# A median search with sixteen marks in six rounds instead of eight marks in eight rounds, in a kernel of three gated norms and a column scan

## The chip, the cores and the metric

One Trainium2 chip, of which this kernel uses one core. The metric is the device time of one execution in microseconds (us), taken as the median of three timed runs. The core has five engines that run their own instruction streams and meet only through semaphores: TensorE (PE in the profile, PEld for its weight loads), VectorE (DVE), ScalarE (ACT), GpSimd (POOL) and SyncE (SP), which here issues all DMAs. Data lie in two on-chip memories of 128 partitions: SBUF, and PSUM, into which TensorE writes and which GpSimd doesn't use here.

## The reference

The input `x` has shape 4 x 1024 x 32 x 32 (images, channels, height, width), in float32. Three times over, `x` is group-normalized, and a gate of one number for each image and channel is computed and applied:

```python
xf = x.reshape(b, c, h * w)
u = jnp.stack([mean(xf), max(xf), std(xf, ddof=1)], axis=-1)   # [4, 1024, 3]
med = jnp.median(u.reshape(b, -1), axis=-1)                   # one per image, over 3072 values
u = (u - med) ** 3
z = jnp.einsum('bck,ck->bc', u, cfc_w) / sqrt(1 + BN_EPS) * bn_w + bn_b
return x * sigmoid(z)                                          # and x = x + this, over _gn(x)
```

Then a fourth layer runs 62 dependent steps over the columns, forward and back: each takes the column before it, multiplies its 1024 channels by a 1024 x 1024 matrix, adds a bias, applies a leaky ReLU and adds the column's own input.

## The kernel before, in words

`x` stays in SBUF as `x_sb[128, 8, 32, 128]`: channel within a tile, 8 channel tiles, 32 columns, 4 images x 32 rows. The execution has three stages.

**Loading, to about 48 us of the profile.** SyncE loads `x` in sixteen pieces of about 1 MB. GpSimd first writes its constants (L330 to L397: identity, group masks, and the constants of the median search), then adds pairs of columns (`pair_add`, L400) as the pieces land; TensorE sums them (L585, L597), VectorE takes maxima (L846), ScalarE sums squares (L469). The weight matrix is loaded behind `x`.

**Three gate layers, 48 to 110 us.** Only the statistics, three numbers per image and channel, are worked on. They lie in `unit[128, 4, 3, 8]`. Each layer runs in a chain: `first_norm` or `next_norm` on VectorE makes `unit`; `median(layer)` finds the median of each image; the cube, the weights and the sigmoid make the gate (L1047 to L1055, L517).

**The scan, from 111 us to the end.** Every column step is 48 large matmuls for the two halves (L680, L683, L686), with weights split into a high part `w_hi` and a low part `w_lo`. The split itself is done inside the gate layers: ScalarE copies the high part (`split_high`, L494), GpSimd subtracts it to make the low part in 24 pieces of a third of a tile (`split_low`, L428), eight per layer. TensorE waits for all 24 at L668 before it warms up for the scan.

**How the median is found.** There are 3072 values for each image. They must stand so that a partition can compare many of them with one threshold. So the statistics are first copied into four columns of `x_sb` that aren't needed then (`COPY_COL`, the last four; SyncE loads them again at L307 once the last layer's values are spread), each value repeated once for every mark: VectorE copies the means (L1042), ScalarE the maxima (L507), GpSimd the deviations (L448). TensorE transposes these columns, 128 values at a time, into PSUM (`ps_values`, L630). After that a partition stands for one pair of image and mark, in one of `SHARES` shares of the channels, and along it lie its values, half of them for ScalarE (`ps_halves[0]`) and half for VectorE (`ps_halves[1]`): `EACH` values for each.

A round then goes like this. ScalarE sums the signs of (threshold - value) over its half (L499, with an accumulator read behind it), VectorE counts the values below the threshold in its half (L998, likewise). GpSimd does one `split_low` beside them. TensorE adds the counts over the partitions that belong to each mark with two small matmuls (L641 waits for ScalarE, L643 for VectorE), and then runs four idle matmuls (`keep_warm`, L578). VectorE compares the sums with half the number of values and adds up the moves of the thresholds (L1009); its signal `thr_ready` starts the next count on both engines, and the next `split_low`. With M marks, a round narrows the interval to 1/M. `SEARCH_WIDTH` is 2.0, and after the last round it is 2 / 8^8.

The last round has another end: one matmul group (`ps_last`, L648 to L656) gives the floors of the two middle ranks, VectorE makes them (L1017, L1019), masks the statistics below each floor (L1022, L1024) and takes the nearest value above (L1026); two small matmuls with a reduction between them give the median to all partitions (L660, L1033, L664).

In layers 1 and 2, three small VectorE operations for the next norm are put into the first three rounds, behind the count (L1002, L1004, L1007). In layer 0, GpSimd folds parameters behind its last `split_low` of that layer (`fold_params`, L431: eight small operations), and VectorE waits for them at L1050.

Of the kernel before, what the change touches and what calls it, by code (L numbers as in the profile page):

```python
# [6 lines left out]
def gated_norm_and_column_scan_kernel(nc, x_cols, w_t, gate_params, conv_bias, prelu_slope, out_cols):  # L7
# [17 lines left out]
    N = 4  # L25
# [21 lines left out]


    SEARCH_LO, SEARCH_WIDTH = -149 / 256, 2.0
    MARKS = 8  # L50
    SHARES = P // (N * MARKS)
    ROUNDS = 8
    STEP = [SEARCH_WIDTH / MARKS ** (k + 1) for k in range(ROUNDS)]
    MARKED = N * MARKS
    TERMS = MARKED + 2
# [8 lines left out]
    with ctx:  # L64
# [86 lines left out]
        both_shift = sb("both_shift", [P, N, CT])  # L151

        spreading = ExitStack()
        ps_values = spreading.enter_context(nc.psum_tensor("ps_values", [P, 2 * 512], fp32))
        spreading.close()
        ps_prods = pb("ps_prods", [P, 2 * HALF])
        ps_prod = [ps_prods[:, c * HALF:(c + 1) * HALF] for c in range(2)]
# [2 lines left out]
        ps_below = pb("ps_below", [P, 2 * 512])  # L160
        ps_group = pb("ps_group", [P, 512])
        ps_means = ps_group[:, N * CT:2 * N * CT]
        ps_cells = [ps_group[:, 128 + 64 * r:128 + 64 * r + TERMS] for r in range(2)]
        ps_last = ps_below[:, 512:512 + 2 * N * (MARKS + 1)]
        ps_second = pb("ps_second", [P, 512])
        ps_var = ps_second[:, 0:N * CT]
# [105 lines left out]

        def copies(k):

            pair = x_sb[:, k, COPY_COL:COPY_COL + 2, :].rearrange("p w m -> p (w m)")
            each = unit[:, :, k, :].rearrange("p n c -> p c n").unsqueeze(3).broadcast_to([P, CT, N, MARKS])
            return pair.rearrange("p (c n j) -> p c n j", n=N, j=MARKS), each

        def copied(t):

            return x_sb[:, t // 2, COPY_COL + t % 2, :]

        moves = stage[:, HALF:HALF + ROUNDS * TERMS].rearrange("p (k t) -> p k t", k=ROUNDS)
        moved = cells[:, 0:TERMS]
        last_moved = tall[:, :, :, :].rearrange("p n k c -> p (n k c)")[:, 0:2 * N * (MARKS + 1)]            .rearrange("p (u n j) -> p u n j", u=2, n=N)
        ps_halves = [ps_values[:, r * 512:r * 512 + EACH] for r in range(2)]

        act_signs = stage[:, 0:EACH // 2].bitcast(bf16)

# [39 lines left out]
        def _(pool):  # L329
# [30 lines left out]
                .then_inc(masks_started, 1)  # L360
            pool.wait_ge(masks_started, 7)
            pool.tensor_tensor(places[:, :], places[:, :], eights[:, :], ALU.mult).then_inc(masks_started, 1)
            pool.tensor_tensor(own[:, :], eights[:, 0:2 * N], eights[:, 2 * N:4 * N], ALU.add).then_inc(masks_started, 1)
            pool.tensor_tensor(cells[:, :], ident[:, 0:2 * MARKED], ident[:, 2 * MARKED:4 * MARKED], ALU.add)\
                .then_inc(masks_started, 1)
            started = 10
            for width in (8, 4, 2, 1):
                pool.wait_ge(masks_started, started)
                pool.tensor_tensor(places[:, 0:width], places[:, 0:width], places[:, width:2 * width], ALU.add)\
                    .then_inc(masks_started, 1)  # L370
                started += 1
            pool.tensor_tensor(own[:, 0:N], own[:, 0:N], own[:, N:2 * N], ALU.add).then_inc(masks_started, 1)
            pool.tensor_tensor(cells[:, 0:MARKED], cells[:, 0:MARKED], cells[:, MARKED:2 * MARKED], ALU.add)\
                .then_inc(masks_started, 1)
            for t in (cell_once, cell_twice):
                pool.memset(t[:, MARKED:TERMS], 0.0).then_inc(consts_ready, 1)
            for t in (last_once, last_twice, next_rank):
                pool.memset(t[:, :, :, :], 0.0).then_inc(masks_started, 1)
            pool.memset(last_moves[:, :, :, :], STEP[-1]).then_inc(consts_ready, 1)
            pool.wait_ge(masks_started, started + 5)  # L380
            by_mark = cells[:, 0:MARKED].rearrange("p (n j) -> p n j", n=N)
            for t, weight in ((cell_once, 1.0), (cell_twice, 2.0)):
                pool.tensor_scalar(t[:, 0:MARKED], cells[:, 0:MARKED], weight, 0.0, ALU.mult, ALU.add)\
# [61 lines left out]
            for layer in range(LAYERS):  # L445

                pool.wait_ge(unit_ready, 2 * layer + 2)
                pool.tensor_copy(*copies(2)).then_inc(pool_copied, 1)  # L448
                pool.wait_ge(spread_high, layer + 1)
                split_low()  # L450
                for k in range(1, ROUNDS):
                    pool.wait_ge(thr_ready, layer * (ROUNDS - 1) + k)
                    split_low()
                if layer == 0:
                    fold_params()

# [2 lines left out]
        def _(act):  # L459
# [35 lines left out]

            def count_signs(layer, k):

                with nc.allow_low_precision(reason="whole numbers up to 384 are exact in float16"):
                    act.activation(act_signs, ps_halves[0], ACT.Sign, bias=moves[:, k, MARKED:MARKED + 1], scale=-1.0,  # L499
                                   accum_out=balance[:, k:k + 1]).then_inc(act_counted, 1)  # L500

# [72 lines left out]
        def _(pe):  # L574
# [28 lines left out]
            for layer in range(LAYERS + 1):  # L603
# [16 lines left out]
                if layer > 0:  # L620
                    keep_warm(6, ps_warm)
                keep_warm(8, ps_warm)
                for t in range(2 * NSTAT):
                    if t == 0:
                        pe.wait_ge(dve_copied, layer + 1)
                    elif t == 2:
                        pe.wait_ge(act_copied, layer + 1)
                    elif t == 4:
                        pe.wait_ge(pool_copied, layer + 1)
                    last = pe.transpose(ps_halves[t // NSTAT][:, t % NSTAT * P:(t % NSTAT + 1) * P], copied(t), ident[:, :])  # L630
                    if t == NSTAT - 1:
                        last.then_inc(spread_low, 1)
                last.then_inc(spread_high, 1)

# [161 lines left out]
        def _(dve):  # L796
# [192 lines left out]
            def median(layer):  # L989

                values = unit[:, :, :, :].rearrange("p n k c -> p n (k c)")

                dve.wait_ge(spread_high, layer + 1)
                for k in range(ROUNDS):
                    if k > 0:
                        dve.wait_ge(thr_ready, layer * (ROUNDS - 1) + k)
                    with nc.allow_low_precision(reason="whole numbers up to 384 are exact in float16"):
                        dve.tensor_scalar(below_flags[:, :], ps_halves[1], moves[:, k, MARKED:MARKED + 1], 0.0,  # L998
                                          ALU.is_lt, ALU.add, accum_out=below[:, k:k + 1]).then_inc(dve_counted, 1)
                    if k < ROUNDS - 1:  # L1000
                        if layer > 0 and k == 0:
                            dve.tensor_tensor(t1[:, 0, :, :], cent[:, 1, :, :], cent[:, 1, :, :], ALU.mult)  # L1002
                        if layer > 0 and k == 1:
                            dve.scalar_tensor_tensor(t2[:, 0, :, :], cent[:, 3, :, :], (PIX - 1.0) / PIX,  # L1004
                                                     cent[:, 3, :, :], ALU.mult, ALU.mult)
                        if layer > 0 and k == 2:
                            dve.tensor_tensor(cent[:, 0, :, :], t1[:, 0, :, :], t2[:, 0, :, :], ALU.add)  # L1007
                        dve.wait_ge(cells_counted, layer * (ROUNDS - 1) + k + 1)
                        dve.scalar_tensor_tensor(moved, ps_cells[k % 2], COUNT_LIMIT, moves[:, k, :],  # L1009
                                                 ALU.is_le, ALU.mult,  # L1010
                                                 accum_out=moves[:, k + 1, MARKED:MARKED + 1]).then_inc(thr_ready, 1)

                dve.wait_ge(lows_given, layer + 1)
                link(dve.tensor_scalar(last_moves[:, :, :, MARKS], ps_lows.unsqueeze(1).broadcast_to([P, 2, N]),
                                       -STEP[-1], None, ALU.add))
                dve.wait_ge(floors_ready, layer + 1)
                link(dve.scalar_tensor_tensor(last_moved, ps_last.rearrange("p (u n j) -> p u n j", u=2, n=N),  # L1017
                                              COUNT_LIMIT, last_moves[:, :, :, :], ALU.is_le, ALU.mult))
                link(dve.tensor_reduce(floors[:, :, :], last_moved, AX.X, ALU.add))  # L1019

                each = values.unsqueeze(1).broadcast_to([P, 2, N, VALUES])
                link(dve.tensor_tensor(spread[:, :, :, :], each,  # L1022
                                       floors[:, :, :].unsqueeze(3).broadcast_to([P, 2, N, VALUES]), ALU.is_lt))
                link(dve.scalar_tensor_tensor(spread[:, :, :, :], spread[:, :, :, :], -BIG, each,  # L1024
                                              ALU.mult, ALU.subtract))
                dve.tensor_reduce(tops[:, :].rearrange("p (u n) -> p u n", u=2),  # L1026
                                  spread[:, :, :, :], AX.X, ALU.max)\
                    .then_inc(tops_ready, 1)
                dve.wait_ge(params_loaded, 48)
                dve.tensor_copy(cube[:, :, NSTAT, :],  # L1030
                                params[:, layer, NSTAT + 1, :].unsqueeze(1).broadcast_to([P, N, CT]))
                dve.wait_ge(tops_turned, layer + 1)
                dve.tensor_reduce(middle[:, :], ps_mid[0:2 * N, 0:P], AX.X, ALU.max).then_inc(median_ready, 1)  # L1033
                dve.wait_ge(median_spread, layer + 1)
# [199 lines left out]
```

## Time and profile before

| | us |
|---|---|
| median of 3 runs (lowest, highest) | 865.32 (865.29, 865.5) |
| the profiled execution, its own time | 865.18 |
| its span, first to last instruction | 863.5 |
| TensorE busy in the span | 840.1 (97%) |
| VectorE busy | 659.0 (76%) |
| ScalarE busy | 412.7 (48%) |
| GpSimd busy | 67.4 (8%), all of it before 102 us |

The granted TensorE clock is 1.000 of full over the span. The scan is TensorE's: busy tenths of 9 in every slice from about 110 us. Between 48 and 110 us the large matmuls don't run yet, and what TensorE is busy with there is mostly `keep_warm`: 173 matmuls of L578, 42.8 us. A timeline row has the start, the duration, the engine, the line, the operation, output <- input, and in brackets the idle time of the engine before it and what ended it. Durations of neighbours on one engine overlap, since an instruction is still finishing when the next one starts; the distance of two starts is what counts.

### The profile page before, as it was taken

Reading aid. Unit: us, or ns where it says so; the run is one execution under the profiler, and the core shown is the slowest. Engines: PE = TensorE matmul, PEld = TensorE weight load, DVE = VectorE, ACT = ScalarE, POOL = GpSimd, SP = SyncE. Lnnn points to the kernel's source line nnn. Section 1 sums busy time; section 2 is a strip of 40 time slices with the busy share of each in tenths; the row PEclk is TensorE's granted clock in tenths of the full one; section 3 lists DMA queues with packets and bytes.
Section 4 is the critical chain, followed back from the end, with each engine's and each line's share of the span. In section 5 each row is a group of like instructions: output and inputs, shape, how many; then the busy total and the mean of one; then the engine's idle time right before and its main releaser. Section 6 shows DMA issues by size and latency. Waiting matters only on the chain.

```text
span 863.5 us, 13836 instructions
## 1 busy us (share of the span) xinstructions
PE 840.1 (97%) x4078; PEld 664.7 (77%) x4078; DVE 659.0 (76%) x1446; ACT 412.7 (48%) x1375; POOL 67.4 (8%) x106
## 2 busy tenths in 40 slices
PE   7788999999999999999999999999999999999998
PEld 7743478888888888888888888888888888888886
DVE  6977787767667676676766787788877888778887
ACT  6964325444454445444454444544445444454444
POOL 8963300000000000000000000000000000000000
PEclk9999999999999999999999999999999999999999
DMA  9940200000000000000000023331333223332233
GB/s 376 418 184 1 97 26 1 0 0 0 0 0 0 0 0 0 0 0 0 0 0 0 15 83 97 97 93 59 92 97 97 87 60 96 97 97 77 68 97 98
DMA packets 70654, 56.34 MB, mean 65 GB/s; under 512 B 1904, under 2 KB 66416, under 8 KB 68720
## 3 DMA queue, kind: packets, MB, share of 16 engines
q1 hardware_dynamic: 70640, 56.17, 19.5%
q8 instruction: 7, 0.11, 0.1%
q14 instruction: 7, 0.06, 0.0%
HBM read 39.39 MB, written 16.78 MB: 65 GB/s over the span
## 4 chain that ended last, share of the span: by engine, by line
PE 89%; POOL 4%; DVE 4%; ACT 2%; issue 1%; POOLq 0%; DVEq 0%
PE ps_prods L680 27%; PE ps_prods L683 27%; PE ps_prods L686 27%; PE ps_turns L702 6%; POOL pairs L400 3%; ACT stage L499 1%; PE ps_below L578 1%; DVE cells L1009 1%; PE ps_below L597 0%; DVE below_flags L998 0%; PE ps_group L641 0%; PE ps_values L630 0%; POOL stage L393 0%; POOL stage L396 0%; PE ps_second L660 0%
## 5 line engine op out<-in xcount | busy, mean ns | idle before, releaser
L680 PE MATMUL ps_prods<-w_hi,s_hi 128*128 128x512 f32 (+1 forms) x1000 | 404.4, 404 | 0.6 <-DVE s_hi L1154 0.6
L683 PE MATMUL ps_prods<-w_lo,s_hi 128*128 128x512 f32 (+1 forms) x1000 | 403.0, 403 | 0.0
L686 PE MATMUL ps_prods<-w_hi,s_lo 128*128 128x512 f32 (+1 forms) x1000 | 392.8, 393 | 0.0
L526 ACT ACTIVATE act_buf<-ps_prods 128x256 f32<-128x256 f32 x247 | 81.5, 382 | 354.4 <-PE ps_prods L686 354.4
L1102 DVE SCALAR_TENSOR_TENSOR x_sb<-act_buf,x_sb 128x256 f32 (+1 forms) x247 | 105.1, 426 | 153.6 <-ACT act_buf L533 143.8
L680 PEld LDWEIGHTS ps_prods<-w_hi,s_hi 128*128 128x128 f32 x1000 | 188.4, 188 | 40.0 <-DVE s_lo L1160 1.3
L686 PEld LDWEIGHTS ps_prods<-w_hi,s_lo 128*128 128x128 f32 x1000 | 188.9, 189 | 38.2
L683 PEld LDWEIGHTS ps_prods<-w_lo,s_hi 128*128 128x128 f32 x1000 | 189.2, 189 | 32.4
L533 ACT ACTIVATE act_buf<-ps_turns,bias 128x128 f32<-128x128 f32 x494 | 156.6, 377 | 51.5 <-PE ps_turns L702 51.5
L539 ACT ACTIVATE ps_below<-ps_turns,neg_bias 128x128 f32<-128x128 f32 x494 | 152.2, 362 | 0.0
L1109 DVE SCALAR_TENSOR_TENSOR x_sb<-ps_below,neg_slope,x_sb 128x256 f32 (+1 forms) x247 | 118.9, 481 | 5.3
L1077 DVE TENSOR_TENSOR s_lo<-x_sb,s_hi 128x256 fp32r<-128x256 f32 x244 | 103.8, 426 | 8.4
L702 PEld LDWEIGHTS ps_turns<-ident,act_buf 128*128 128x128 f32 x494 | 69.0, 140 | 33.1
L702 PE MATMUL ps_turns<-ident,act_buf 128*128 128x128 f32 x494 | 93.9, 272 | 0.0
L1071 DVE TENSOR_SCALAR s_hi<-x_sb 128x256 fp32r (+1 forms) x244 | 70.8, 290 | 4.2
L578 PE MATMUL ps_below<-ones_bf 128*128 128x512 bf16 x173 | 42.8, 379 | 0.0
L1142 DVE TENSOR_TENSOR x_sb<-x_sb,stage 128x1024 f32 (+1 forms) x31 | 38.0, 1225 | 3.2
L1135 DVE TENSOR_TENSOR stage<-stage,a_shift 128x1024 f32<-128x1024 f32 x31 | 38.0, 1225 | 1.1
L1065 DVE TENSOR_TENSOR x_sb<-x_sb,g_shift 128x1024 f32 (+1 forms) x31 | 38.0, 1225 | 1.1
L1062 DVE TENSOR_TENSOR x_sb<-x_sb,g_scale 128x1024 f32 (+1 forms) x31 | 37.8, 1219 | 0.0
L1132 DVE TENSOR_TENSOR stage<-stage,a_scale 128x1024 f32<-128x1024 f32 x31 | 37.8, 1218 | 0.0
L846 DVE TENSOR_REDUCE half_max<-x_sb 128x4 f32<-128x2048 f32 (+1 forms) x16 | 35.4, 2214 | 0.0
(186 smaller groups left out, 342.1 us busy)
## 6 DMA issues: line engine op xcount, KB each, us to landing
stage<-x_cols SPq DMA_DIRECT2D x31, 512.0 KB, 4.1
out_cols<-x_sb SPq DMA_DIRECT2D x31, 512.0 KB, 4.8
x_sb<-x_cols SPq DMA_DIRECT2D x15, 1024.0 KB, 18.6
w_raw<-w_t SPq DMA_DIRECT2D x8, 512.0 KB, 19.4
x_sb<-x_cols SPq DMA_DIRECT2D x1, 2048.0 KB, 8.2
x_sb<-x_cols SPq DMA_DIRECT2D x2, 512.0 KB, 27.1
out_cols<-x_sb SPq DMA_DIRECT2D x4, 128.0 KB, 2.1
params<-gates SPq DMA_DIRECT2D x1, 60.0 KB, 14.3
```

Of the source, the lines that this page charges most:

```text
L526: act.activation(act_buf[:, half], ps_prod[c if bank is None else bank][:, half], ACT.Copy) .then_inc(raw_copied, 1)
L533: last = act.activation(act_buf[:, (2 * r + j) * P:(2 * r + j + 1) * P], ps_turn[r][:, j * P:(j + 1) * P], ACT.Identity, bias=bias[:, ct:c ...
L539: last = act.activation(ps_below[:, r * 512 + j * P:r * 512 + (j + 1) * P], ps_turn[r][:, j * P:(j + 1) * P], ACT.Relu, bias=neg_bias[:, c ...
L578: pe.matmul(bank[:, :], ones_bf[:, :], ones_bf[:, :].unsqueeze(1).broadcast_to([P, 4, P]), start=True, stop=True)
L680: pe.matmul(out, s_hi[:, k, :], w_hi[:, k, w_cols], start=(k == 0), stop=False)
L683: pe.matmul(out, s_hi[:, k, :], w_lo[:, k, w_cols], start=False, stop=False)
L686: return pe.matmul(out, s_lo[:, k, :], w_hi[:, k, w_cols], start=False, stop=(k == CT - 1))
L702: last = pe.transpose(ps_turn[r][:, j * P:(j + 1) * P], act_buf[:, q * P:(q + 1) * P], ident[:, :])
L1071: dve.tensor_scalar(s_hi[:, ct0:ct0 + 2, :], pair, 1.0, None, ALU.mult)\
L1077: dve.tensor_tensor(s_lo[:, ct0:ct0 + 2, :], pair, s_hi[:, ct0:ct0 + 2, :].bitcast(fp32), ALU.subtract).then_inc(state_ready, 1)
L1102: dve.scalar_tensor_tensor(col, y, 0.0, col, ALU.max, ALU.add).then_inc(above_added, 1)
L1109: dve.scalar_tensor_tensor(col, below, neg_slope[:, 0:1], col, ALU.mult, ALU.add)\
```

## The change

`MARKS` goes from 8 to 16, `ROUNDS` from 8 to 6. The final interval is the same, 2 / 16^6 = 2 / 8^8. Everything sized by them follows:

- `SHARES` goes from 4 to 2, `EACH` from 384 to 768, `TERMS` from 34 to 66, `STEP` has six entries.
- The copies are 128 x 512 for each statistic instead of 128 x 256, over all four columns of `COPY_COL`, and there are twelve transposes in each layer instead of six; `ps_values` takes four PSUM banks of 512 instead of two, ScalarE's half starting at 0 and VectorE's at 1024. `spread_low` is signalled behind the sixth transpose, `spread_high` behind the twelfth.
- `ps_last`, `last_moves`, `last_once` and the like are 136 wide instead of 72. `last_moved` moves from `tall` to `spread`.
- GpSimd's constants: `places` is added up in three steps instead of four, `own` and `cells` lose their second addition, and there are ten instructions for `moves` (L393, L396) instead of fourteen.
- GpSimd's eight pieces of `w_lo` per layer stay eight. Six of them are still started by the rounds; the other two follow directly behind the sixth, in a new loop, in layer 0 ahead of `fold_params`.

```diff
-    MARKS = 8
+    MARKS = 16
-    ROUNDS = 8
+    ROUNDS = 6
...
-        ps_values = spreading.enter_context(nc.psum_tensor("ps_values", [P, 2 * 512], fp32))
+        ps_values = spreading.enter_context(nc.psum_tensor("ps_values", [P, 4 * 512], fp32))
...
-        ps_cells = [ps_group[:, 128 + 64 * r:128 + 64 * r + TERMS] for r in range(2)]
+        ps_cells = [ps_group[:, 128 + 128 * r:128 + 128 * r + TERMS] for r in range(2)]
...
-            pair = x_sb[:, k, COPY_COL:COPY_COL + 2, :].rearrange("p w m -> p (w m)")
+            pair = x_sb[:, k, COPY_COL:COLS, :].rearrange("p w m -> p (w m)")
...
-            return x_sb[:, t // 2, COPY_COL + t % 2, :]
+            return x_sb[:, t // 4, COPY_COL + t % 4, :]
...
-        ps_halves = [ps_values[:, r * 512:r * 512 + EACH] for r in range(2)]
+        ps_halves = [ps_values[:, r * 1024:r * 1024 + EACH] for r in range(2)]
...
-            pool.tensor_tensor(own[:, :], eights[:, 0:2 * N], eights[:, 2 * N:4 * N], ALU.add).then_inc(masks_started, 1)
-            pool.tensor_tensor(cells[:, :], ident[:, 0:2 * MARKED], ident[:, 2 * MARKED:4 * MARKED], ALU.add)\
+            pool.tensor_tensor(own[:, 0:N], eights[:, 0:N], eights[:, N:2 * N], ALU.add).then_inc(masks_started, 1)
+            pool.tensor_tensor(cells[:, 0:MARKED], ident[:, 0:MARKED], ident[:, MARKED:2 * MARKED], ALU.add)\
...
-            for width in (8, 4, 2, 1):
+            for width in (4, 2, 1):
...
                 for k in range(1, ROUNDS):
                     pool.wait_ge(thr_ready, layer * (ROUNDS - 1) + k)
                     split_low()
+                for _ in range(W_THIRDS // LAYERS - ROUNDS):
+                    split_low()
                 if layer == 0:
                     fold_params()
...
-                for t in range(2 * NSTAT):
+                half = EACH // P
+                for t in range(2 * half):
                     if t == 0:
                         pe.wait_ge(dve_copied, layer + 1)
-                    elif t == 2:
+                    elif t == 4:
                         pe.wait_ge(act_copied, layer + 1)
-                    elif t == 4:
+                    elif t == 8:
                         pe.wait_ge(pool_copied, layer + 1)
-                    last = pe.transpose(ps_halves[t // NSTAT][:, t % NSTAT * P:(t % NSTAT + 1) * P], copied(t), ident[:, :])
-                    if t == NSTAT - 1:
+                    last = pe.transpose(ps_halves[t // half][:, t % half * P:(t % half + 1) * P], copied(t), ident[:, :])
+                    if t == half - 1:
                         last.then_inc(spread_low, 1)
                 last.then_inc(spread_high, 1)
```

## Rows read from the trace of the kernel before

**Rows 1.** The page, its chain that ended last: shares of the span by engine.
```profile
PE 89%; POOL 4%; DVE 4%; ACT 2%; issue 1%; POOLq 0%; DVEq 0%
```

**Rows 2.** Timeline, one round of layer 2: start us, duration us, engine, line, operation.
```profile
99.31 0.20 DVE L1009 SCALAR_TENSOR_TENSOR cells<-ps_group,stage 128x34 f32<-128x34 f32 x1 [0.35 <-PE ps_group L643]
...
99.55 0.58 ACT L499 ACTIVATE stage<-ps_values,stage 128x384 bf16<-128x384 f32 x1 [0.54 <-DVE cells L1009]
99.55 0.62 DVE L998 TENSOR_SCALAR_CACHE_REDUCE below_flags<-ps_values,stage 128x384 uint8<-128x384 f32 x1
...
100.03 0.20 ACT L499 ACTIVATION_READ_ACCUMULATOR stage<-ps_values,stage 128x1 f16 x1
100.09 0.09 DVE L998 DVE_READ_ACCUMULATOR below_flags<-ps_values,stage 128x1 f16 x1
...
100.53 0.19 DVE L1009 SCALAR_TENSOR_TENSOR cells<-ps_group,stage 128x34 f32<-128x34 f32 x1 [0.35 <-PE ps_group L643]
```

**Rows 3.** Timeline, the start of the search in layer 1.
```profile
71.79 0.29 DVE L1042 COPY x_sb<-unit 128x256 f32<-128x256 f32 x1
...
71.94 0.40 POOL L448 COPY x_sb<-unit 128x256 f32<-128x256 f32 x1 [6.70 <-DVE unit L838]
...
72.16 0.84 PE L630 MATMUL ps_values<-ident,x_sb 128*128 128x128 f32 x6
...
73.13 0.62 DVE L998 TENSOR_SCALAR_CACHE_REDUCE below_flags<-ps_values,stage 128x384 uint8<-128x384 f32 x1 [0.76 <-PE ps_values L630]
...
73.67 0.09 DVE L998 DVE_READ_ACCUMULATOR below_flags<-ps_values,stage 128x1 f16 x1
...
74.05 0.20 DVE L1009 SCALAR_TENSOR_TENSOR cells<-ps_group,stage 128x34 f32<-128x34 f32 x1
```

**Rows 4.** Groups by line and shape: busy us, mean ns of one.
```profile
L1030 DVE COPY cube<-params 128x32 f32<-128x32 f32 x3 | 0.6, 186 | 0.0
...
L1042 DVE COPY x_sb<-unit 128x256 f32<-128x256 f32 x3 | 0.9, 287 | 0.0
...
L1077 DVE TENSOR_TENSOR s_lo<-x_sb,s_hi 128x256 fp32r<-128x256 f32 x244 | 103.8, 426 | 8.4
...
L1135 DVE TENSOR_TENSOR stage<-stage,a_shift 128x1024 f32<-128x1024 f32 x31 | 38.0, 1225 | 1.1
...
L930 DVE TENSOR_TENSOR grow<-gate,rstd 128x32 f32<-128x32 f32 x3 | 0.6, 192 | 0.9 <-ACT gate L517 0.9
...
L469 ACT ACTIVATE ps_prods<-x_sb,mean_div 128x1024 f32<-128x1024 f32 x16 | 17.6, 1098 | 0.0
```

**Rows 5.** Timeline, the end of the search in layer 2.
```profile
100.81 0.91 POOL L428 TENSOR_TENSOR w_lo<-w_raw,w_hi 128x342 fp32r<-128x342 f32 x1 [0.30 <-DVE cells L1009]
...
101.84 0.23 DVE L1017 SCALAR_TENSOR_TENSOR tall<-ps_below,last_moves 128x72 f32<-128x72 f32 x1 [0.36 <-PE ps_below L656]
102.11 0.23 DVE L1019 TENSOR_REDUCE floors<-tall 128x8 f32<-128x72 f32 x1
102.37 0.36 DVE L1022 TENSOR_TENSOR spread<-unit,floors 128x192 f32<-128x192 f32 x1
```

**Rows 6.** Timeline, GpSimd and VectorE side by side, in layer 0 and layer 2.
```profile
64.03 0.38 POOL L437 TENSOR_SCALAR neg_bias<-bias 128x8 f32<-128x8 f32 x1
...
93.50 0.91 POOL L428 TENSOR_TENSOR w_lo<-w_raw,w_hi 128x342 fp32r<-128x342 f32 x1 [0.33 <-DVE cells L1009]
...
94.00 0.46 DVE L1004 SCALAR_TENSOR_TENSOR t<-cent 128x32 f32<-128x32 f32 x1
```

**Rows 7.** Timeline of GpSimd alone, the loading stage.
```profile
9.46 0.22 POOL L393 TENSOR_SCALAR stage<-own 128x32 f32<-128x32 f32 x1
...
10.02 0.22 POOL L393 TENSOR_SCALAR stage<-own 128x32 f32<-128x32 f32 x1
...
26.77 19.77 POOL L400 TENSOR_TENSOR pairs<-x_sb 128x1024 f32<-128x1024 f32 x9 [1.19 <-DMA x_sb<-x_cols]
```

**Rows 8.** Busy time in one stretch: PE, PEld, DVE, ACT, POOL, then granted clock, DMA share, GB/s.
```profile
23.40:29.30 5.90, 4.10 (x33) 3.75 (x33) 5.90 (x5) 4.56 (x9) 4.58 (x3) 1.00 1.01 417
```

More of the change, by code:

```diff
@@ L279, in copied @@
         def copied(t):
[L281 removed]
+            return x_sb[:, t // 4, COPY_COL + t % 4, :]
         moves = stage[:, HALF:HALF + ROUNDS * TERMS].rearrange("p (k t) -> p k t", k=ROUNDS)
         moved = cells[:, 0:TERMS]
[L285 to L286 removed]
+        last_moved = spread[:, :, :, :].rearrange("p u n v -> p (u n v)")[:, 0:2 * N * (MARKS + 1)]\
+            .rearrange("p (u n j) -> p u n j", u=2, n=N)
+        ps_halves = [ps_values[:, r * 1024:r * 1024 + EACH] for r in range(2)]
         act_signs = stage[:, 0:EACH // 2].bitcast(bf16)
@@ L371, in _ @@
                 started += 1
-            pool.tensor_tensor(own[:, 0:N], own[:, 0:N], own[:, N:2 * N], ALU.add).then_inc(masks_started, 1)
-            pool.tensor_tensor(cells[:, 0:MARKED], cells[:, 0:MARKED], cells[:, MARKED:2 * MARKED], ALU.add)\
-                .then_inc(masks_started, 1)
             for t in (cell_once, cell_twice):
@@ L379, in _ @@
             pool.memset(last_moves[:, :, :, :], STEP[-1]).then_inc(consts_ready, 1)
-            pool.wait_ge(masks_started, started + 5)
+            pool.wait_ge(masks_started, started + 3)
             by_mark = cells[:, 0:MARKED].rearrange("p (n j) -> p n j", n=N)
@@ L496, in count_signs @@
             def count_signs(layer, k):
-                with nc.allow_low_precision(reason="whole numbers up to 384 are exact in float16"):
+                with nc.allow_low_precision(reason="whole numbers up to 768 are exact in float16"):
                     act.activation(act_signs, ps_halves[0], ACT.Sign, bias=moves[:, k, MARKED:MARKED + 1], scale=-1.0,
@@ L996, in median @@
                         dve.wait_ge(thr_ready, layer * (ROUNDS - 1) + k)
-                    with nc.allow_low_precision(reason="whole numbers up to 384 are exact in float16"):
+                    with nc.allow_low_precision(reason="whole numbers up to 768 are exact in float16"):
                         dve.tensor_scalar(below_flags[:, :], ps_halves[1], moves[:, k, MARKED:MARKED + 1], 0.0,
```

## The prediction

> **What bounds the kernel now.** I read the chain that ended last first: TensorE has 89% of it, and GpSimd, VectorE and ScalarE share the rest [rows 1]. The 89% is the scan, which the change doesn't touch: what matters is when it starts. I therefore went to the timeline of the gate layers. There the work is a chain across engines, none of them full, and each step starts when the one before it ends. In a round [rows 2] the reader is to see both counts start at 99.55, ScalarE's done at 100.23 (100.03 + 0.20) and VectorE's at 100.18; the sums come back to L1009 at 100.53, and the next count starts 0.24 us after L1009 (99.31 to 99.55). A round is 1.22 us (99.31 to 100.53), of which the count is 0.68. Everything that lengthens this chain moves the end of the kernel one to one, since TensorE waits for the gate before it can start the scan. So the change is judged by the length of three searches.
>
> Times below go by the profiled execution, 865.18 us (span 863.5); the median of the runs is 865.32, 0.14 above it.
>
> **The counts.** Each count reads 768 values instead of 384. What does a value more cost? On VectorE, 1024 against 256 elements take 1225 against 426 ns [rows 4]: 1.04 ns each, so +0.40 us. The count's own row gives the upper bound, 0.62 us over 384, 1.6 ns each, +0.62 us [rows 2]; the lower bound is the rate of the copies, 0.45 ns (186 ns for 32, 287 ns for 256 elements, [rows 4]), +0.17 us. I take 1.04, because the count reads PSUM and its 0.54 us to the accumulator read is hardly to be had at the copy's rate. On ScalarE, a sum over 1024 elements takes 1098 ns [rows 4], the count over 384 580 ns [rows 2]: 0.81 ns each, I take +0.32 us (upper bound 1.5 ns from the count's row alone, +0.58).
>
> VectorE then ends its count 0.63 + 0.40 = 1.03 us after the start, ScalarE 0.68 + 0.32 = 1.00. They are near level, and VectorE becomes the later one. From the end of VectorE's count to L1009, where it is the last, takes 0.29 us (73.76 to 74.05, [rows 3]). The matmuls are 66 columns instead of 34, for which I add 0.01, and L1009 has 32 elements more, 0.03. A round becomes 1.03 + 0.29 + 0.01 + 0.24 + 0.03 = 1.60 us.
>
> **One layer, step by step.**
> - Copy (L1042): 256 elements more at 0.45 to 0.53 ns, +0.13 us [rows 4]; it stands before the first transpose. ScalarE's and GpSimd's copies grow too, but are wanted only at the fifth and ninth transpose. GpSimd's lasts 0.40 us now and ends at 72.34 [rows 3]; even doubled it ends at 72.74, while the ninth transpose starts about 0.13 + 8 x 0.11 us after 72.16, at 73.2. Cost nothing; uncovered it would be 0.4 at most.
> - Transposes: six take 0.84 us with 0.27 for the last alone, a distance of 0.11 us [rows 3]. Six more: +0.68. VectorE waits for the last one, as it does now at 73.13.
> - First count, to the first L1009: +0.40 + 0.01 = +0.41.
> - Six distances from L1009 to L1009 at 1.22 go (7.31 in all), four at 1.60 come (6.40): -0.91.
> - Last count: from the last L1009 to L1017. Now 1.31 us (100.53 to 101.84, [rows 2, 5]). ScalarE's end moves by 0.32 and VectorE's end by 0.40 from a start 0.05 earlier, so +0.35; 0.03 for L1009; the matmuls with 136 columns are within this rounding: +0.38.
> - L1017 and L1019 have 64 elements more each, 0.067 us each: +0.13.
>
> Sum: 0.13 + 0.68 + 0.41 - 0.91 + 0.38 + 0.13 = +0.82 us for a layer, +2.5 for three. Two rounds are saved, 2.4 us, but six counts cost 0.32 to 0.40 more each, and the wider copy and transposes 0.8. This is the main term.
>
> **GpSimd's two late pieces.** The change leaves the eight pieces of `w_lo` and starts three of them at the last `thr_ready`. The last count starts at 100.77 (L1009 at 100.53 [rows 2] plus 0.24). Now the last piece starts 0.04 us after it and is over at 101.72, before L1017 [rows 5]. Three at 0.91 end at 0.04 + 2.73 = 2.77 us after the count's start. VectorE reaches L1022 after 1.60 us now (102.37 - 100.77), with the terms above after 1.60 + 0.35 + 0.13 = 2.08 us: in the middle of the third piece. What happens when a VectorE instruction meets one of these, [rows 6] show: L1004, a 32-element instruction whose like takes 192 ns alone [rows 4], takes 0.46 us, and ends at 94.46, 0.05 after the GpSimd piece at 94.41. I found six such meetings (L1002, L1004, L1007 and the L838 that writes `rstd`, in layers 1 and 2, the first three with `w_lo`), and all end 0.04 to 0.05 us behind GpSimd. The counts run beside the pieces undisturbed: L998 has 0.62 us with a piece beside it from its start [rows 2]. So L1022 waits. It ends at 2.77 + 0.05 + 0.17 (160 elements more than the 32 of those rows) = 2.99 us instead of 2.08 + 0.36 = 2.44: +0.55. GpSimd's pieces may overlap by some 0.04 each in their records, which would make it 0.47; I take +0.5 for each layer, +1.5. At the least it costs nothing (rival below). At the most the third piece itself starts late behind L1017 and pushes the rest by another 0.3, +0.8 for each layer.
>
> The Trainium skill (SBUF — State Buffer, "Who interferes with whom") states that a VectorE instruction with two SBUF inputs contends with a GpSimd instruction that reads SBUF, and that the later one is blocked for the whole instruction, while reductions and instructions with one SBUF input are left alone. By that, L1017 (one input from PSUM) and L1019 (a reduction) pass and L1022 is the one that waits; the six meetings agree, since all have two SBUF inputs. If L1017 waited as well, the end of the third piece would still set L1022, and the sum would stay.
>
> In layer 0 `fold_params` now comes behind the third piece, eight small instructions. L1022 and L1024 run there, and one waits for the other: L437, 8 elements, took 0.38 us beside L1022 [rows 6]. I add 0.15 us once. The fold ends some 2 us behind the third piece, near 4.9 us after the last count's start; L1052, which needs it, comes at about 5.4 us, so it is just covered; uncovered it would be up to 0.5 once.
>
> **The constants.** GpSimd saves four `moves` instructions, 0.56 us for a pair (9.46 to 10.02, [rows 7]), and three small additions, 1.7 us, less some 0.5 for wider ones. It reaches its first `pair_add` about 1 us sooner, and the chain that ended last runs through it. But at 26.77 GpSimd had sat idle for 1.19 us until a piece of `x` landed [rows 7], and it can't start that piece before it has landed: that swallows the gain. I take 0, bounds 0 and -1.0.
>
> **Other covers.** `w_lo` is complete at about 104.7 + 0.8 us in layer 2, and TensorE asks for it behind the last gate, at 107.5 now: covered. The reload of four columns of `x` starts later with the last transpose and has 8.2 us to land; it is wanted after 111. Cost nothing.
>
> **Sum.** 865.18 + 2.5 + 1.5 + 0.15 = 869.3 in the profiled execution; the median of the runs stands 0.14 above it, so **869.4 us**, 0.47% slower.
>
> **The rivals.**
> - B, no lock: the pieces never meet L1022, because they overlap more or the counts are longer. Then the searches cost 2.5 us alone: 867.7. For it: three meetings with `w_lo` are few, all with small instructions. Against: all agree, and the times overlap by 0.7 us.
> - C, rounds with a fixed price (the other side): if a count of 768 cost no more than one of 384, two saved rounds would come through. For it: of 0.62 us some is start-up. A layer would be 0.13 + 0.68 + 0.01 - 2.44 (two rounds) + 0.16 (the wider L1009 and matmuls), and the end at L1022 still hangs on the third piece, 2.99 us against 1.96 now, +1.03: -0.43, so 865.18 - 1.3 + 0.15 = 864.0; without the lock 861.5. It decides below +0.09 us for a count with the lock and +0.2 without; the rates of both engines [rows 2, 4] say 0.3 to 0.4.
> - D, the clock falls: a longer round leaves TensorE about 0.5 us idle behind its four warm-up matmuls, where it was 0.1. If the granted clock fell to 1.2 GHz in the searches, twelve transposes would cost 1.3 us more and the small matmuls 0.2: +1.5 a layer, 871 in one layer to 874 in all. Against: in the loading stage TensorE was busy 4.10 of 5.90 us, and the granted clock was 1.00 [rows 8]; the new round has about 1.2 of 1.6.
> - E, the constants' gain comes through: 868.3. Against it stands the idle time on the DMA.
>
> **How the numbers follow.** My forecast 0.62, B 0.18, E 0.08, D 0.08, C 0.04. What can be told from no change is 0.2%, 1.7 us to either side of 865.32. B, D and E lie above it. Slower 0.92, within 0.2% 0.05 (half of C and counts cheaper than I think), faster 0.03. The range reaches down past B and leaves out C, up to the lock's upper bound and a clock that falls in one layer: 867.3 to 870.9.
>
> **What would show it.** In the profile after: L998 at about 1.02 us and L499 at 0.90; L1009 to L1009 at 1.60; twelve transposes in 1.5 us; from L1042 to L1017 0.7 us more than the 10.87 of now (71.79 to 82.66); L1022 longer than 0.8 us, ending 0.2 behind a GpSimd piece; the clock at 1.00. L998 below 0.8 us would make the forecast wrong on the side of C, L1022 at 0.36 us on that of B.

## The result, and the profile after

The changed kernel takes 870.91 us (median of four executions, 869.52 to 871.78), the kernel before 865.31: a ratio of 1.0062, 95% interval 1.0048 to 1.0075. (The ratios here are estimated from all the executions, so they can differ a little from the quotient of two medians, which is 1.0065 here.) It is slower by 5.6 us. The profiled execution is the fastest of the four, 869.52 us with a span of 867.8, 4.34 us above the one of before. Its granted clock was 1.000; the other three had 0.996, 0.994 and 0.996 over their span. So there are two things to explain: 4.3 us in the profile, and 1.4 more in the median.

To read the first, one stretch is taken out of each trace: from VectorE's first copy of statistics in layer 0 (L1042 before, L1043 after) to its first instruction of the scan (L1150 before, L1151 after). It holds the three searches and nothing of the loading or the scan. Before, it is 57.47 us (52.67 to 110.14); after, 61.24 us (52.64 to 113.88). That is 3.77 us. The load ended at the same moment, and the rest, 0.6 us, lies in the scan, where nothing was changed. The two ends of the stretch, in the timeline of the kernel before:

```profile
52.67 0.28 DVE L1042 COPY x_sb<-unit 128x256 f32<-128x256 f32 x1
...
110.14 0.29 DVE L1150 TENSOR_TENSOR stage<-x_sb,g_scale 128x128 f32<-128x128 f32 x1
```

and in that of the changed kernel:

```profile
52.64 0.42 DVE L1043 COPY x_sb<-unit 128x512 f32<-128x512 f32 x1
...
113.88 0.29 DVE L1151 TENSOR_TENSOR stage<-x_sb,g_scale 128x128 f32<-128x128 f32 x1
```

One round of layer 2, in the timeline of the changed kernel, to be laid beside [rows 2]:

```profile
98.50 0.23 DVE L1010 SCALAR_TENSOR_TENSOR cells<-ps_group,stage 128x66 f32<-128x66 f32 x1 [0.20 <-PE ps_group L644]
...
98.77 0.90 ACT L499 ACTIVATE stage<-ps_values,stage 128x768 bf16<-128x768 f32 x1 [0.60 <-DVE cells L1010]
98.78 1.02 DVE L999 TENSOR_SCALAR_CACHE_REDUCE below_flags<-ps_values,stage 128x768 uint8<-128x768 f32 x1
...
99.57 0.20 ACT L499 ACTIVATION_READ_ACCUMULATOR stage<-ps_values,stage 128x1 f16 x1
99.72 0.09 DVE L999 DVE_READ_ACCUMULATOR below_flags<-ps_values,stage 128x1 f16 x1
...
100.10 0.23 DVE L1010 SCALAR_TENSOR_TENSOR cells<-ps_group,stage 128x66 f32<-128x66 f32 x1 [0.20 <-PE ps_group L644]
```

From L1010 to L1010 it is 1.60 us (98.50 to 100.10), and VectorE (99.81) is now later than ScalarE (99.77). The 384 values more cost VectorE 0.40 us and ScalarE 0.32.

The start of the search in layer 1, against [rows 3]:

```profile
73.01 0.42 DVE L1043 COPY x_sb<-unit 128x512 f32<-128x512 f32 x1
...
73.16 0.74 POOL L446 COPY x_sb<-unit 128x512 f32<-128x512 f32 x1 [6.07 <-DVE unit L839]
...
73.49 1.53 PE L631 MATMUL ps_values<-ident,x_sb 128*128 128x128 f32 x12
...
75.14 1.02 DVE L999 TENSOR_SCALAR_CACHE_REDUCE below_flags<-ps_values,stage 128x768 uint8<-128x768 f32 x1 [1.19 <-PE ps_values L631]
```

The twelve transposes take 1.53 us instead of 0.84, and VectorE sits idle for 1.19 us in front of its count instead of 0.76. GpSimd's copy is done at 73.90 and delays nothing.

The end of the search in layer 1, against [rows 5]:

```profile
83.17 2.64 POOL L426 TENSOR_TENSOR w_lo<-w_raw,w_hi 128x341 fp32r<-128x341 f32 x3 [0.68 <-DVE cells L1010]
...
84.57 0.30 DVE L1018 SCALAR_TENSOR_TENSOR spread<-ps_below,last_moves 128x136 f32<-128x136 f32 x1 [0.34 <-PE ps_below L657]
84.91 0.29 DVE L1020 TENSOR_REDUCE floors<-spread 128x8 f32<-128x136 f32 x1
85.23 0.78 DVE L1023 TENSOR_TENSOR spread<-unit,floors 128x192 f32<-128x192 f32 x1
...
86.85 0.39 PE L661 MATMUL ps_second<-ident,tops 128*8 128x128 f32 x2 [0.88 <-DVE tops L1027]
```

GpSimd's three pieces end at 85.81. L1023 has the same 192 elements as L1022 before, at 0.36 us; here it takes 0.78 and ends at 86.01, 0.20 behind GpSimd. L1018 and L1020 passed through the same pieces and show only their 64 elements more.

The loading stage: GpSimd's first additions start 0.9 us sooner, at 10.71, and it is stopped by DMAs again at 24.30, where before it was stopped at 26.77 [rows 7].

```profile
10.71 12.31 POOL L398 TENSOR_TENSOR pairs<-x_sb 128x1024 f32<-128x1024 f32 x5 [0.32 <-DMA x_sb<-x_cols]
24.30 22.22 POOL L398 TENSOR_TENSOR pairs<-x_sb 128x1024 f32<-128x1024 f32 x10 [1.28 <-DMA x_sb<-x_cols]
```

### The profile page after: what moved, and what is told of

Its sections match the earlier page's. It is cut to its first block, busy times and chain, and to the rows that moved or that the text cites. A ratio compares the mean times of both kernels' runs of the same rounds, so it can differ in the third digit from the quotient of the medians.

```text
span 867.8 us, 13745 instructions
## 1 busy us (share of the span) xinstructions
PE 837.1 (96%) x4060; PEld 664.2 (77%) x4060; DVE 662.8 (76%) x1422; ACT 416.0 (48%) x1363; POOL 67.4 (8%) x99
## 4 chain that ended last, share of the span: by engine, by line
PE 89%; DVE 3%; POOL 3%; ACT 2%; DMA 1%; issue 1%; SPq 0%; POOLq 0%; DVEq 0%
PE ps_prods L681 27%; PE ps_prods L687 27%; PE ps_prods L684 27%; PE ps_turns L703 6%; POOL pairs L398 3%; ACT stage L499 2%; DMA x_sb<-x_cols 1%; PE ps_below L578 1%; PE ps_values L631 1%; PE ps_below L597 0%; DVE cells L1010 0%; DVE below_flags L999 0%; PE ps_group L642 0%; DVE spread L1023 0%; SPq L299 0%
## 5 line engine op out<-in xcount | busy, mean ns | idle before, releaser
L578 PE MATMUL ps_below<-ones_bf 128*128 128x512 bf16 x149 | 36.8, 379 | 0.0
```

The source lines that it names most:

```text
L578: pe.matmul(bank[:, :], ones_bf[:, :], ones_bf[:, :].unsqueeze(1).broadcast_to([P, 4, P]), start=True, stop=True)
```

## The experiments

Chips differ here: the median of the kernel before is 864.9 or 865.0 us on two of them and 866.1 to 866.4 on a third, mostly at a granted clock of 0.999 or 1.000. So each time is given with the kernel before on the same chip (866.06 and 866.39 are two sets on the third). The stretch is the one defined above, in the profiled execution.

| kernel | median us | before, same chip | ratio (95%) | stretch us | executions with a clock under 0.999 |
|---|---|---|---|---|---|
| changed, again | 870.02 | 866.06 | 1.0047 (1.0034 to 1.0061) | 61.25 | 3 of 5 |
| five idle matmuls | 869.55 | 866.06 | 1.0039 (1.0025 to 1.0052) | 61.24 | 1 of 5 |
| piece moved ahead | 868.75 | 866.06 | 1.0036 (1.0023 to 1.0050) | 60.82 | 5 of 5 |
| both | 867.44 | 864.93 | 1.0029 (1.0017 to 1.0040) | 59.98 | 1 of 7 |
| half the counts | 863.66 | 864.93 | 0.9985 (0.9976 to 0.9994) | 56.12 | 1 of 10 |
| and six transposes | 861.56 | 864.93 | 0.9960 (0.9945 to 0.9976) | 54.15 | 0 of 4 |
| before, pieces late | 867.43 | 864.93 | 1.0027 (1.0017 to 1.0037) | 59.90 | 0 of 8 |
| before, two idle matmuls | 869.01 | 866.06 | 1.0034 (1.0022 to 1.0046) | 59.91 | 6 of 6 |
| three idle matmuls | 869.60 | 866.39 | 1.0043 (1.0030 to 1.0056) | 62.97 | 2 of 6 |
| two in the last round | 868.87 | 864.97 | 1.0045 (1.0031 to 1.0059) | 61.27 | 2 of 5 |
| all three mendings | 867.33 | 864.97 | 1.0028 (1.0017 to 1.0038) | 59.94 | 0 of 8 |

**Half the counts.** Both engines read 384 of the 768 values; the other half of the values is left out of all comparisons.

```diff
-act.activation(act_signs, ps_halves[0], ACT.Sign, ...
+act.activation(act_signs[:, 0:EACH // 2], ps_halves[0][:, 0:EACH // 2], ACT.Sign, ...
-dve.tensor_scalar(below_flags[:, :], ps_halves[1], ...
+dve.tensor_scalar(below_flags[:, 0:EACH // 2], ps_halves[1][:, 0:EACH // 2], ...
```

> The changed kernel with both counts over the first 384 of their 768 values; the other half of the values is left out of every comparison, so the medians are wrong. All else (twelve transposes, 512-wide copies, 66 and 136 columns, pieces) stays. Theory 1: a round falls from 1.60 to 1.27 us (four of them), the first count by 0.40, and the last count gives nothing, since L1023 hangs on the third GpSimd piece: 1.7 us for each layer, 5.2 in all, 864.4. Theory 1 without the hold-up at the end: 2.07 a layer, 863.3. Rival C (a count costs the same whatever its length): 869.5.

The stretch is 5.12 us shorter than in the changed kernel, where 5.2 was expected with the hold-up at the end and 6.2 without. The timeline of layer 0 shows both sides: a round is 1.27 us (56.94 to 58.21), and L1023 takes 1.10 us. It arrives sooner and waits longer for the same GpSimd piece. (The row of POOL shows the last two of the three pieces, since this view starts at 62.)

```profile
56.94 0.23 DVE L1010 SCALAR_TENSOR_TENSOR cells<-ps_group,stage 128x66 f32<-128x66 f32 x1 [0.37 <-PE ps_group L644]
...
58.21 0.23 DVE L1010 SCALAR_TENSOR_TENSOR cells<-ps_group,stage 128x66 f32<-128x66 f32 x1 [0.37 <-PE ps_group L644]
...
61.93 1.78 POOL L426 TENSOR_TENSOR w_lo<-w_raw,w_hi 128x341 fp32r<-128x341 f32 x2
...
62.82 1.10 DVE L1023 TENSOR_TENSOR spread<-unit,floors 128x192 f32<-128x192 f32 x1
```

**And six transposes.** The same, and of each half only the three transposes that are still read.

```diff
+if t % half >= half // 2:
+    continue
 last = pe.transpose(...)
-if t == half - 1:
+if t == half // 2 - 1:
     last.then_inc(spread_low, 1)
```

> As the kernel with half the counts, and only the six transposes whose values are still read (the copies stay 512 wide; half the values are left out of every comparison). Theory 1: 6 x 0.11 = 0.68 us less for each layer, 2.0 us under the kernel with half the counts, 862.3. Rival (transposes hide beside other work): no difference between the two.

1.97 us less in the stretch, 2.10 in the medians. The transposes lie bare on the chain, at 0.11 us each.

**Piece moved ahead.** The test of GpSimd's part in the changed kernel.

```diff
 pool.tensor_copy(*copies(2)).then_inc(pool_copied, 1)
+split_low()
 pool.wait_ge(spread_high, layer + 1)
 split_low()
...
-for _ in range(W_THIRDS // LAYERS - ROUNDS):
+for _ in range(W_THIRDS // LAYERS - ROUNDS - 1):
```

> The changed kernel with one of GpSimd's two late pieces started behind its copy, ahead of the wait for the transposes. Two pieces are left at the last round; they end 1.8 us after the last count's start, 0.3 before VectorE asks for L1023. Theory 1 with the lock: L1023 at 0.36 us instead of 0.78, 0.42 to 0.46 us less in each layer, 868.2 at clock 1.000. Rival (the pieces have no part in it, the time is all in the wider steps): 869.5 as before. Theory 2b (clock falls through the idle TensorE at the end of the search, which shrinks from 0.9 to 0.45 us) expects the spread over executions to go; 2a expects it to stay.

L1024 (the L1023 of the changed kernel) is back at 0.36 us in all layers:

```profile
L1024 DVE TENSOR_TENSOR spread<-unit,floors 128x192 f32<-128x192 f32 x3 | 1.1, 359 | 0.1
```

The stretch fell by 0.43 us only, though, since in this profiled execution the clock fell in layer 1 (its rows stand under three idle matmuls, below). With the clock held (the run "both", below) it is 59.98, 1.26 under the changed kernel: 0.42 for each layer. The clock fell in all five executions, so the shorter idle time at the end of the search (theory 2b) did not keep it up.

**Before, pieces late.** The same thing put into the kernel before.

```diff
 pool.wait_ge(thr_ready, layer * (ROUNDS - 1) + k)
-split_low()
+if k not in (5, 6):
+    split_low()
+for _ in range(2):        # behind the loop over k
+    split_low()
```

> The kernel before the change, with the GpSimd pieces of rounds 5 and 6 put behind the one of the last round, so that three run in a row there, as in the changed kernel; nothing else is altered. Theory 1 with the lock: the third piece ends 2.68 us after the last count's start, and L1022 ends 0.21 behind it at 2.89 instead of 1.96: 0.93 us for each layer, 2.8 in all, some 0.15 more in layer 0, 868.2 at clock 1.000. Rival (no lock): 865.3. Theory 2b expects here a granted clock below 1.000 in some executions, since TensorE idles about 1.3 us at the end of each search.

+2.43 us in the stretch, +2.50 in the medians: 0.81 for each layer where I expected 0.93. The rows of layer 0 show why it is a little less. GpSimd began 0.15 us later than usual; L1025 (the old L1022) got in as the second piece ended, the third piece had to wait for it, and it was the next instruction, L1027, that then waited for the third piece:

```profile
62.93 2.76 POOL L428 TENSOR_TENSOR w_lo<-w_raw,w_hi 128x342 fp32r<-128x342 f32 x3 [2.90 <-DVE cells L1012]
...
64.34 0.58 DVE L1025 TENSOR_TENSOR spread<-unit,floors 128x192 f32<-128x192 f32 x1
64.96 0.94 DVE L1027 SCALAR_TENSOR_TENSOR spread<-spread,unit 128x192 f32<-128x192 f32 x1
```

Theory 2b alone is out: TensorE idled for 1.13 us at the end of the search here, and the clock was 0.999 or 1.000 in all eight executions. So an idle end of the search does not bring the clock down by itself, with rounds of 1.22 us.

**The changed kernel once more, and the clock.**

> The changed kernel once more, unaltered. Theory 1 (the sum: counts, transposes, copies and a VectorE instruction held up by GpSimd's late pieces give a fixed +4.3 us) expects 869.5 in every execution whose granted clock is 1.000. Theory 2 (the clock falls in some executions, because TensorE now idles about 0.5 us in each round and 0.9 us at the end of a search) expects single executions at 870.5 to 872 with a mean clock of 0.993 to 0.997, and others at 869.5 with 1.000. If all five are within 0.3 us of each other, theory 2 has no ground here.

Executions took 869.58, 871.2, 870.08, 869.58 and 870.02 us, at clocks of 1.000, 0.994, 0.998, 1.000 and 0.998. The lower clock goes with the longer time, as in the first four. At 0.997 and 0.998 that is not so in every kernel: with five idle matmuls the execution at 0.998 took 869.43 us, where those at 1.000 took 869.55 to 869.63.

**Before, two idle matmuls.** `keep_warm(4, ps_warm)` in the rounds becomes `keep_warm(2, ps_warm)`, in the kernel before.

> The kernel before the change with two idle matmuls in each round instead of four, so TensorE idles about 0.65 of 1.22 us in each round, more than in the changed kernel. Theory 2a (idle time in the rounds lets the clock fall): executions 1 to 8 us above 865.3, mean clock below 1.000 in some or all. If the clock stays at 1.000 and the time at 865.3, idle time in rounds isn't the cause in the changed kernel either.

All six executions have clocks of 0.990 to 0.994 and are 2.95 us slower in the median. TensorE's rows of layer 0 show the fall: two idle matmuls take 0.59 us, then 1.01, while the engine did nothing else than this same pattern (timeline of that kernel):

```profile
57.23 0.59 PE L578 MATMUL ps_below<-ones_bf 128*128 128x512 bf16 x2
...
58.46 1.01 PE L578 MATMUL ps_below<-ones_bf 128*128 128x512 bf16 x2
```

The search in layer 0 of the same kernel by windows, with columns as in [rows 8], has a mean clock of 0.84: at 1.2 GHz for a part of it (0.50 from 58.40 to 61.00) and at 2.4 for the rest.

```profile
53.00:63.50 10.50, 7.49 (x40) 2.54 (x41) 6.62 (x32) 5.39 (x16) 7.61 (x9) 0.84 0.02 7
58.40:61.00 2.60, 2.30 (x11) 0.49 (x12) 1.66 (x8) 1.35 (x4) 1.94 (x3) 0.50 0.00 0
```

**Five idle matmuls.** `keep_warm(4, ps_warm)` becomes `keep_warm(5, ps_warm)` in the changed kernel.

> The changed kernel with five idle matmuls behind each round's sums instead of four. They end 0.23 us before ScalarE's count is there, so the round stays at 1.60 us. Theory 2a (the idle 0.49 us in each round makes the clock fall): all executions at clock 1.000 and 869.5. Theory 2b (the idle 0.9 us at the end of each search does it) or 2c (it falls elsewhere): the same spread as the changed kernel, 869.5 to 872.

Five executions within 0.27 us (869.36 to 869.63), the profile's stretch unchanged at 61.24: the fifth matmul costs nothing.

**Three idle matmuls.** The other direction, `keep_warm(3, ps_warm)`.

> The changed kernel with three idle matmuls in each round instead of four, so TensorE idles about 0.75 of 1.60 us. Theory 2a (idle time in the rounds lets the clock fall): now nearly every execution has a mean clock of 0.99 to 0.995 and takes 871 to 873.5 us, 2 to 4 above the changed kernel's 869.5, and the profile shows stretches below 1.00 between 53 and 110 us. If it has the same mix as the changed kernel (some executions at 1.000 and 869.5), the number of idle matmuls isn't what decides.

This was missed. Two of six executions fell, to 0.994 and 0.990 (871.28 and 872.68 us); four stayed at 1.000 and 869.4 to 869.6. A low mean clock went down to 0.990, where the lowest with four was 0.994, but it was not more frequent. The profiled execution is one of the two. By windows of this kernel, with columns as in [rows 8], TensorE was busy 1.64 of 3.90 us up to the end of the last round of layer 0, and the clock was 1.00 there; in the 3.60 us behind it was 0.62:

```profile
60.00:63.90 3.90, 1.64 (x11) 0.73 (x10) 3.23 (x11) 2.69 (x6) 2.52 (x4) 1.00 0.00 0
63.90:67.50 3.60, 3.46 (x12) 1.03 (x12) 2.52 (x10) 0.01 (x1) 3.28 (x10) 0.62 0.02 5
```

By the transposes of the next layer it was back: they take 1.53 us, as at full clock. All three searches of this execution fell in this way at their end, so that the seven idle matmuls behind the last count took 2.51, 3.00 and 3.15 us instead of 1.67 (timeline of TensorE, this kernel):

```profile
64.09 2.51 PE L578 MATMUL ps_below<-ones_bf 128*128 128x512 bf16 x7
...
74.25 1.53 PE L631 MATMUL ps_values<-ident,x_sb 128*128 128x128 f32 x12
...
85.08 3.00 PE L578 MATMUL ps_below<-ones_bf 128*128 128x512 bf16 x7
...
106.18 3.15 PE L578 MATMUL ps_below<-ones_bf 128*128 128x512 bf16 x7
```

The same windows in layer 1 of the kernel with the piece moved ahead show the same fall:

```profile
80.00:83.50 3.50, 1.85 (x12) 0.82 (x11) 2.83 (x9) 2.30 (x6) 2.12 (x3) 0.97 0.00 0
83.50:87.30 3.80, 3.56 (x12) 1.29 (x12) 2.06 (x9) 0.19 (x2) 1.01 (x2) 0.58 0.00 0
```

TensorE's rows in the timeline of that kernel, behind its last count in layer 1:

```profile
83.94 3.03 PE L579 MATMUL ps_below<-ones_bf 128*128 128x512 bf16 x7
86.91 0.38 PE L662 MATMUL ps_second<-ident,tops 128*8 128x128 f32 x2
```

They show how the fall gets into the time: the seven idle matmuls behind the last count take 3.03 us (83.94 to 86.97) instead of the 1.67 they have at full clock, and L662, which VectorE waits for, stands behind them. In the stretch this fall cost 0.84 us (60.82 against the 59.98 of the run "both"), and the three falls of the kernel with three idle matmuls cost 1.73 (62.97 against 61.24).

**Two in the last round.** The last round is the one without idle matmuls. `keep_warm(2, ps_warm)` is put behind the matmul of `lows_given`, nothing else.

> The changed kernel with two idle matmuls more in each layer, in the last round only, behind the matmul of the lowest marks; the other rounds keep four. They fill 0.5 of the 0.65 us for which TensorE waits for the last count. Theory 2d (the clock falls at the end of a search, because the last round is the one without idle matmuls; in the two profiles with a fall it set in there): all executions at clock 0.999 or 1.000 and 869.5. Theory 2a (the idle time of the five other rounds decides): the mix of the changed kernel stays, some executions at 0.994 to 0.998 and 870 to 871.8.

Two of five executions still have a clock of 0.997, but their times (868.75 and 868.87) are those of the others at 0.999 (868.91 and 868.79). The longest, 869.68, is the profiled one, at 1.000. So filling the last round does not keep the clock up by itself; whether it took away the fall's price is left open by five executions.

**Both, and all three mendings.** Five idle matmuls and the moved piece; then the two in the last round as well.

> Both edits at once: five idle matmuls in a round, and one late GpSimd piece moved ahead of the transposes. Theory 1 and 2a together: every execution near 868.2, with a spread below 0.4 us and clock 1.000, that is 1.3 to 1.4 us under the changed kernel with five idle matmuls. If the spread of the kernel with the moved piece (868.5 to 870.4) stays, 2a is wrong.

> All three mendings: one GpSimd piece ahead of the transposes, five idle matmuls in each round, two in the last. Theories 1 and 2 (a or d): the search is 1.26 us shorter than in the changed kernel, 868.2 where the kernel before takes 865.3, in all executions, clock 1.000. It stays slower than the kernel before by the counts, transposes and copies, 2.5 us; if it came within 0.5 us of it, the term of the widths would be wrong.

867.44 and 867.33 us, that is 2.5 and 2.4 above the kernel before on the same chip. The second has eight executions within 0.4 us. In the first, two of seven lie at 868.4 and 868.5, one of them at a clock of 1.000; that one's extra time is in the scan.

## Why the prediction was right, and where it was not

**Right in direction and in the work that is added; the median lies at the edge of the range.** The range was 867.3 to 870.9, and the median is 870.91. The forecast of 869.4 is the time of the undisturbed executions (869.52, and 869.58 twice in the second set); the median came out 1.5 above it because the clock fell in three of four executions, and that it did not come out above the range is luck. There is some luck in the profiled execution too: forecast 869.3, measured 869.52, but the searches gave 0.38 less than forecast and the scan, for which nothing was forecast, 0.56 more. Of 3.77 us in the stretch the prediction had 4.15. Step by step:

- *The counts.* L999 at 1.02 us and L499 at 0.90, rounds of 1.60: as predicted. That the price is the length of the count is shown by half the counts, 5.12 us against 5.2. Rival C is refuted.
- *Copy, transposes and rounds together.* From L1043 to L1018 in layer 1 it is 11.56 us (73.01 to 84.57) against 10.87, +0.69 where 0.69 was forecast. Up to the first count (L999) it is 2.13 us (73.01 to 75.14) against 1.34: 0.79 for the copy and the transposes, where 0.81 was forecast.
- *L1018 and L1020.* +0.13 (0.66 instead of 0.53 us to the start of L1023), as forecast.
- *GpSimd's pieces.* The mechanism was right and refutes B; it was mis-sized. 0.42 us a layer by the trace and by the moved piece, where I took 0.5: the three pieces last 2.64 us together, not 2.73. In layer 0, the fold cost 0.04 on L1025 instead of 0.15. The evidence was stronger than the prediction says: the trace of before has eight meetings that end 0.04 to 0.05 us behind GpSimd, not six, and six of them are with `w_lo` (L1002, L1004 and L1007, in layers 1 and 2).
- *The constants.* Nothing came through: the first copy starts at 52.64 instead of 52.67. E is refuted in this trace.
- *Slips that decide nothing.* By its own terms rival C without the lock is 861.2, not 861.5. The 0.27 us of the last transpose is in the trace of before (272 to 273 ns for most, L630), but not in [rows 3]. And `w_lo` is complete at 106.25 (103.61 + 2.64) and not near 105.5, still 5 us ahead of the scan's first matmuls.

0.69 + 0.13 + 0.42 is 1.24 for a layer; three of them with the 0.04 make 3.76 of the 3.77.

**Wrong about the clock.** One of the signs asked for was "the clock at 1.00"; it holds for one of the first four executions. The step that failed is the one on rival D: "Against: in the loading stage TensorE was busy 4.10 of 5.90 us, and the granted clock was 1.00 [rows 8]". A stretch at 1.00 in one execution said nothing about the others. With four idle matmuls in rounds of 1.60 us, 13 of 19 executions were below 0.999, counting the five with two more in the last round, and 11 of 14 without these; with five, 2 of 20; in the kernel before, whose four matmuls fill rounds of 1.22 us, 3 of 52. The kernels did not all run on one chip; on the one chip that had both, it was 8 of 10 with four and 1 of 5 with five. The executions at 0.996 took 1.3 to 1.4 us more than the one at 1.000, the one at 0.994 took 2.3 more (870.86, 870.96 and 871.78 against 869.52). This is the greater part of what the median has over 869.4.

D gave the fall 8 in 100 and priced it at 1.5 us for a layer, through transposes at the low clock. Size and way were others: in the two profiles of kernels with sixteen marks that show a fall, all transposes take 1.53 us, and a fall costs 0.84 us once and 1.73 in three layers, through the seven idle matmuls that stand ahead of a matmul that VectorE waits for. No execution of the changed kernel that fell was profiled, so that it fell in the same place is likely, not shown.

**Not explained.** 0.6 us of the profile's 4.34 lies in the scan (753.92 us from L1151 to the end, 753.36 before). Over the profiles of the other kernels at a clock of 1.000 this part has between 752.88 and 753.88 us, and the kernel before itself has single executions 1.4 us apart on one chip at 1.000 (864.70 and 866.13). I count it as the scatter of the scan; its source was not sought. For the same reason the difference of whole times depends on where it is taken: on the chip of the second set the changed kernel at 1.000 is 3.5 us above the median of the kernel before (869.58 against 866.06), with the same stretch of 61.25. Why three idle matmuls fell less often than four (2 of 6 on a chip where four had 8 of 10) is open as well; by theory 2a it should have been more often. So it is shown that the number of idle matmuls in a round matters (two in the kernel before: 6 of 6, against 1 of 10 on the same chip), and not by what rule.

**What the change costs at its best.** With both side effects mended, the wider counts, copies and transposes leave 2.4 us (1.0028, 1.0017 to 1.0038), the 2.5 of the main term. The experiments point to no version with sixteen marks that beats the kernel before: in each layer the two rounds saved are 2.4 us (2 x 1.22), and the 0.38 us by which each of the six others is longer take 2.3 of them back before the copy and the transposes are paid.

## What to carry to other kernels

In a chain of short rounds, split the round into what is paid once (here 0.54 us for sums, comparison and signals, 0.57 after the change) and what grows with the data (0.68, to 1.03), and count fewer rounds against wider ones with both, with everything that prepares the wider data (copy and transposes, 0.8 us) on the bill. Work that one engine did beside a round loses its place when rounds are removed: look at which instruction of the neighbour it meets then, and put it where that neighbour reads PSUM or waits. And when a round gets longer, refill what kept TensorE busy in it, and look at the granted clock of every execution, since the one that is profiled may be the one where it held. Look also at where idle matmuls stand right ahead of one that another engine waits for: a row of seven that ends in time at full clock (1.67 us) was what a low clock (3.03) made the chain wait for.

## What the runs showed of the hardware

- A VectorE instruction with two SBUF inputs that meets a GpSimd `tensor_tensor` ends with it: 192 elements took 0.78 us (83.17 + 2.64 to 86.01) or 1.10 us instead of 0.36, ending 0.20 to 0.21 us behind (86.01 against 85.81). The Trainium skill (SBUF — State Buffer, "Who interferes with whom") has the first to start hold the ports for its whole instruction; the trace agrees, and adds that with GpSimd's instructions back to back VectorE can get in between two of them and hold up the next, as in the pieces put late into the kernel before (three pieces at 2.76 us instead of 2.64, and 0.94 us for L1027 where it has 0.36 alone).
- The same pieces do not touch counts from PSUM (1.02 us in all 18) or a reduction (L1020, 0.29 us).
- TensorE's granted clock fell from 2.4 to 1.2 GHz in the midst of a pattern that it had held for several rounds (two idle matmuls a round in the kernel before, 0.59 us and then 1.01). In the changed kernel it fell in some executions and not in others. Executions with a mean clock under 0.999 were 11 of 14 with four idle matmuls a round and 2 of 20 with five, one more of 0.22 us (1.03 against 0.81 for four and three); but 2 of 6 with three, so this is no rule in the number of them.
